# A retention and FP4 feed-forward kernel on one core: its opening, up to the third step, written out anew

## What is computed

```python
Q = _xpos(X @ W_Q);  K = _xpos(X @ W_K, downscale=True);  V = X @ W_V
scores = jnp.einsum('bqd,bkd->bqk', Q, K)
p_attn = jax.nn.softmax(scores, axis=-1) * 0.9 ** jnp.abs(n - m)
x = _layernorm(X + jnp.einsum('bqk,bkv->bqv', p_attn, V))

def fp4_quant_dequant(x):          # blocks of 16 along the last dim
    scale = jnp.maximum(jnp.max(jnp.abs(xb), axis=-1, keepdims=True) / 6.0, 1e-12)
    idx = jnp.searchsorted(_MID, jnp.abs(xb / scale))
    return _GRID[idx] * jnp.sign(xb / scale) * scale
# fp4_linear(x, w): einsum('bsk,nk->bsn', quantised x, quantised w)
h = jax.nn.silu(fp4_linear(x, w_gate)) * fp4_linear(x, w_up)
x = _layernorm(x + fp4_linear(h, w_down))
```

## Time and profile before

| | us |
|---|---|
| median of 3 runs (1080.03 to 1081.76) | 1081.22 |
| the profiled execution | 1081.23 |
| its span, from the first to the last instruction | 1079.4 |

### The profile page before, as it was taken

How to read it: one execution, slowest core, us unless ns; L and a number is a source line. 1 busy time by engine, 2 the same in 40 slices (tenths; PEclk the granted TensorE clock), 3 DMA queues, 4 the chain that set the end, 5 groups by cost and what they waited for, 6 DMA issues and landing times.

```text
span 1079.4 us, 20103 instructions
## 1 busy us (share of the span) xinstructions
PE 1017.5 (94%) x6756; PEld 950.8 (88%) x6756; DVE 888.1 (82%) x1762; ACT 577.0 (53%) x1395; POOL 753.6 (70%) x975
## 2 busy tenths in 40 slices
PE   5559999999999999999999999999999999999974
PEld 4448899999999999999999999999999999999964
DVE  6956888878888888888888888888888888888873
ACT  3233565556555565655555556645556565565543
POOL 3563786878777687868768687867767787666652
PEclk9769999999999999999999999999999999999987
DMA  5210010211012010211012010200111110000000
GB/s 189 81 63 26 11 59 21 69 40 60 16 36 79 20 55 16 80 40 51 19 41 78 12 59 21 78 31 20 60 40 54 35 60 20 16 20 21 21 11 20
DMA packets 28182, 47.24 MB, mean 44 GB/s; under 512 B 2864, under 2 KB 21552, under 8 KB 26032
## 3 DMA queue, kind: packets, MB, share of 16 engines
q1 hardware_dynamic: 27264, 45.17, 12.7%
q10 hardware_dynamic: 816, 0.79, 0.2%
HBM read 37.55 MB, written 8.39 MB: 43 GB/s over the span
## 4 chain that ended last, share of the span: by engine, by line
PE 86%; DVE 7%; issue 3%; POOL 1%; ACT 1%; DMA 1%; SPq 0%; POOLq 0%; DVEq 0%; ACTq 0%
PE ps_g L401 11%; PE ps_g L403 11%; PE ps_g L402 11%; PE ps_t L410 9%; PE ps_o L401 6%; PE ps_o L402 5%; PE ps_o L403 5%; PE ps_s L401 5%; PE ps_s L403 5%; PE ps_s L402 5%; PE ps_y L401 3%; PE ps_y L403 3%; PE ps_y L402 3%; PE ps_y L410 1%; DMA decay_t<-w_up 1%
## 5 line engine op out<-in xcount | busy, mean ns | idle before, releaser
L1291 POOL TENSOR_TENSOR h<-h,hsc 128x64 f32<-128x64 f32 (+3 forms) x257 | 204.0, 815 | 145.5 <-DVE h L1126 115.9
L401 PE MATMUL ps_g<-wgu_h,xqt_h 128*128 128x352 f32 x512 | 173.2, 338 | 2.7 <-DVE h L1097 1.7
L403 PE MATMUL ps_g<-wgu_h,xqt_l 128*128 128x352 f32 x512 | 165.6, 324 | 0.0
L402 PE MATMUL ps_g<-wgu_l,xqt_h 128*128 128x352 f32 x512 | 165.6, 323 | 0.0
L1455 POOL TENSOR_TENSOR prob<-prob,decay_t 128x512 f32<-128x512 f32 x128 | 162.8, 1292 | 3.1 <-ACT prob L782 3.1
L401 PE MATMUL ps_o<-v_h,pt_h 128*128 128x256 f32 x512 | 150.5, 294 | 5.8 <-DVE pt_l L962 5.8
L403 PE MATMUL ps_o<-v_h,pt_l 128*128 128x256 f32 x512 | 145.6, 284 | 0.0
L402 PE MATMUL ps_o<-v_l,pt_h 128*128 128x256 f32 x512 | 145.5, 284 | 0.0
L782 ACT ACTIVATE prob<-ps_s,nmax 128x1024 f32<-128x1024 f32 x64 | 71.3, 1114 | 87.0 <-DVE nmax L1158 87.0
L401 PE MATMUL ps_s<-k_h,q_h 128*128 128x512 f32 x256 | 107.6, 420 | 9.9 <-DVE k_l L1072 9.9
L1089 DVE SCALAR_TENSOR_TENSOR th<-th,ps_g 128x352 f32<-128x352 f32 x128 | 66.7, 521 | 57.4 <-ACT th L712 55.9
(11 more groups left out here) (195 smaller groups left out, 3072.7 us busy)
## 6 DMA issues: line engine op xcount, KB each, us to landing
rope_t<-rope SPq DMA_DIRECT2D x16, 1024.0 KB, 5.2
xin<-x_t SPq DMA_DIRECT2D x16, 512.0 KB, 4.0
xres<-x SPq DMA_DIRECT2D x64, 128.0 KB, 2.0
out<-yout SPq DMA_DIRECT2D x64, 128.0 KB, 1.7
decay_t<-decay SPq DMA_DIRECT2D x1, 960.0 KB, 4.8
h<-w_down SPq DMA_DIRECT2D x2, 352.0 KB, 4.5
prob<-w_k ACTq DMA_DIRECT2D x1, 256.0 KB, 3.3
prob<-w_q ACTq DMA_DIRECT2D x1, 256.0 KB, 4.9
```

Of the source, the lines that this page charges most:

```text
L401: pe.matmul(dst, a_h, b_h, start=(start and i == 0), stop=False)
L402: pe.matmul(dst, a_h, b_l, start=False, stop=False)
L403: mm = pe.matmul(dst, a_l, b_h, start=False, stop=(stop and i == n - 1))
L1291: return tt(blocks(dst), blocks(src), sc[:, which, at:at + n].unsqueeze(2).to_broadcast([P, n, QB]), ALU.mult)
```

## The change

The opening is written out anew up to the start of step 3. From there on each engine's instructions are the ones of before in the same order; the steps are now numbered straight through from 0 to 68 in place of a batch and a tile. What is new before step 3:

- Five homes in SBUF for the first loads, which share their bytes with halves of K and V that are written later (`sb_before` gives a tensor and frees its place at once): `w_first`, `w_last`, `w_down`, `rope_first`. The first sequence's K and V go into the other half (`half_of`). The first x chunk is split into `pt_h` and `pt_l`, the second is loaded into `x1`. SP issues all loads without a wait, gate and up rows of block 0 ahead of x.
- The weights are five blocks: 0, 1, 2 of 2 x 128 rows of gate and up (1024 columns, the last with 64 rows of padding), 3 and 4 of `w_down` (704 columns). POOL does all scalings of them.
- The magnitudes go to PSUM, into the two banks of `ps_o` and `ps_y`, now one tensor `ps_oy`. `wmag` is gone.
- The three first rotations have banks and buffers of their own (`ps_g`, `ps_s`, `ps_t`), the products with the sine stay in PSUM for two of them. DVE turns Q and the second K, POOL the first K; POOL makes all low parts of them.
- The weight transposes go to `ps_g`, in place of `ps_o` and `ps_y`, between the first scores, projections and value products.

```diff
-        w_buffers = [decay_t[:, 0:2 * D], decay_t[:, 2 * D:4 * D], x1_flat[:, 0:2 * D], x1_flat[:, 2 * D:4 * D],
-                     xin[:, 0], xin[:, 1], h[:, 0, 0:F], h[:, 1, 0:F]]
-        rot_borrowed = (prob[:].rearrange("p (a n) -> p a n", a=2), h[:, :, 0:CW])
-        w_magnitudes = [wmag[:], th_flat]
+        def sb_before(name, shape):
+            with nc.sbuf_tensor(name, shape, F32) as t:
+                return t
+        w_first = sb_before("first_gate_up", [P, 2, 2, 2 * D])
         k_h = sb("k_h", [P, 2 * DH * L], F32R)
+        w_last = sb_before("last_gate_up", [P, 2, 2 * D])
         k_l = sb("k_l", [P, 2 * DH * L], F32R)
+        w_down = sb_before("first_down", [P, 2, FP])
         v_h = sb("v_h", [P, 2 * NT * D], F32R)
+        rope_first = sb_before("first_rope", [P, 4, CW])
...
+        first_bank = (ps_g[:], ps_s[:], ps_t_pair)
+        first_cos = (rot_a[:], h[:, :, 0:CW], prob[:].rearrange("p (a n) -> p a n", a=2))
+        first_sin = (rot_b[:], ps_s[:], ps_t_pair)
+        def w_magnitude(m):
+            return ps_oy[:, :, 0:CW if m < 3 else FH]
+        def w_bank(g):
+            return ps_g[:, g % 2].rearrange("p (a n) -> p a n", a=4)
...
+            load_gate_up(0)
+            sp.dma_start(xin[:], x_chunks[0]).then_inc(first_x_arrived[0], 16)
+            load_gate_up(1)
+            sp.dma_start(first_table[0], rope[0][:, 2:4]).then_inc(first_rope_arrived[0], 16)
+            sp.dma_start(first_table[1], rope[0][:, 0:2]).then_inc(first_rope_arrived[1], 16)
+            load_last_gate_up()
+            sp.dma_start(rope_t[:], rope[1]).then_inc(rope_in, 16)
             sp.dma_start(ident[:], ident_in).then_inc(ident_arrived, 16)
-            load_chunk(Batch(0), 0)
-            sp.dma_start(rope_t[:], rope[0]).then_inc(rope_in, 16)
-            load_weights(0)
-            load_weights(1)
-            sp.wait_ge(xtl_done, 1)
-            load_chunk(Batch(0), 1)
...
+            sp.dma_start(w_down[:, :, 0:F], wd.rearrange("(u p) n -> p u n", p=P)).then_inc(w_arrived[3], 16)
             sp.dma_start(decay_t[:], decay).then_inc(decay_arrived, 16)
...
+            project(1, first_bank[0], first_xt[0], first_p_done[0])
+            pe.wait_ge(wqkvl_done, 2)
+            project(0, first_bank[1], first_xt[0], first_p_done[1])
+            pe.wait_ge(first_xl_done[1], 1)
+            project(1, first_bank[2], first_xt[1], first_p_done[2])
+            pe.wait_ge(wqkvl_done, 3)
+            pe.wait_ge(first_mul_done[0], 2)
+            values(first_v_bank[0], first_xt[0], first_p_done[3])
+            scores(0, 0)
+            pe.wait_ge(ident_arrived, 16)
+            weight_transposes(0)
+            weight_transposes(1)
+            scores(0, 1)
+            pe.wait_ge(first_rot_done[2], 2)
+            values(first_v_bank[1], first_xt[1], first_p_done[4])
+            pe.wait_ge(wtl_done, 2)
+            project_next(0, 1)
+            scores(1, 0)
+            scores(1, 1)
...
+            for s in range(OPEN, TILES + LAG):
+                step(s)
...
+            first_weight_high(0)
+            first_x_high(0)
+            weight_magnitude(0)
+            first_weight_high(1)
+            first_x_high(1)
+            first_weight_high(2)
...
+                wait(pe, xqtl_done, i + 1)
+                wait(pe, h_done, 2 * i + r)
```

More of the change, by code:

```diff
@@ L254, in build @@
         block = ctx.enter_context(nc.Block())
[L256 to L271, removed]
-                return 1, K_STEP[j], 1, 2 * K_STEP[j]
-            if j == 0:
-                return 0, 1, 0, 3
-            if j in Q_STEP and batch.has_next() and j > 0:
-                return 0, 0, 1, 1
-            return None
@@ L392, in _ @@
+            for s in range(TILES + LAG):
+                step(s)
             sp.wait_ge(out_stored, 16 * TILES)
@@ L514, in projection, with step @@
+            gate_up(0, 1)
+            def step(s):
+                now, prev, gu, dn, fin = (s - lag for lag in range(5))
+                rot, c_v = rotation(s), values_chunk(s)
+                def projection():
+                    wait(pe, h_done, 2 * dn + 2)
                     if rot is not None:
-                        which, c, on, _ = rot
-                        wait(pe, xtl_done, batch.lin(2, 2 * on + c + 1))
-                        project(which, k_done if which else q_done)
+                        project_next(*rot)
@@ L645, in weight_high, with weight_magnitude @@
+            def weight_magnitude(m):
+                act.wait_ge(wn_done, m + 1)
+                wait(act, wgrid_done, m)
+                nc.scalar.activation(w_magnitude(m), w_values(m), ACT.Abs, scale=MAGIC).then_inc(wabs_done, 1)
             def weight_high(g):
@@ L828, in step @@
+            rotated_high(0, 1)
+            probs_high(1, 0)
+            probs_high(1, 1)
+            x_magnitude(0)
+            exponential(2)
+            x1_high(0)
+            r1_mean(1)
+            r1_squares(1)
+            tanh(0, 0)
+            def step(s):
+                now, prev, gu, dn, fin, end = (s - lag for lag in range(6))
+                turned, c_v, c_x = rotation(s - 1), values_chunk(s), split_chunk(s)
+                urgent = rotation_is_urgent(s)
                 if c_v is not None and urgent:
@@ L1263, in _ @@
+                second_residual(fin)
+                x_max(prev)
+                h_low(dn)
+                x_scales(prev)
+            for s in range(OPEN, TILES + LAG):
+                step(s)
         @block.gpsimd
@@ new lines, in rotated_low @@
+            def rotated_low(which, c):
+                wait(pool, kqh_done, rotation_count(which, c) + 1)
+                if which:
+                    for a in range(DH):
+                        at = half_of(c // 2) * (DH * L) + a * L + (c % 2) * CW
+                        ins = tt(k_l[:, at:at + CW], rot_a[:, a, :], k_h[:, at:at + CW].bitcast(F32), ALU.subtract)
+                else:
+                    ins = tt(q_l[:, c % 2], rot_a[:], q_h[:, c % 2].bitcast(F32), ALU.subtract)
+                ins.then_inc(kql_done, 1)
```

1773 lines of the change are left out of this document (924 added, 849 removed).

## The result

| | before | after |
|---|---|---|
| median of 4 runs, us | 1081.49 (1080.03 to 1082.27) | 1055.59 (1054.66 to 1056.68) |
| profiled execution, us | 1081.23 | 1054.66 |
| its span, us | 1079.4 | 1052.8 |
| first score product of tile 3, us | 97.96 | 70.99 |
| from there to the end of the span, us | 981.4 | 981.8 |

The ratio is 0.9762, 95% interval 0.9745 to 0.9779: 25.9 us faster. Forecast were 1055.7 us and the range 1050 to 1065. The number is met; two of its terms, the start of step 3 and the stretch behind it, were off by some 2 us each, in opposite directions, as the experiments show. That it comes out within 0.1 us is in part luck.

What follows compares the result with a forecast made beforehand. The opening was taken as bound by the DVE and POOL chain quantising weights and rotating keys and queries, the body by PE. Step 3 moves from 97.96 to 72.5, so 1081.2 - 25.5 = 1055.7 us, range 1050 to 1065.

Steps and rivals of the forecast that it cites:

- the start of step 3: First score product of tile 3, ending the opening: 70.5 us by the sum, 72.5 with allowance, against 97.96 before.
- Loads: Start of the opening: x is split at 7.4 us instead of 5.73, a loss of 1.7; later loads cost nothing.
- The lock: Opening: POOL's operations hold DVE's with both inputs in SBUF; 4.4 us lost after 11.0, magnitudes in PSUM escape.
- Rival (a): Opening: POOL's locks catch DVE oftener, 8.3 us more, time 1064 us; chance 0.14.
- DVE's queue up to the row maximum: Opening from 11.0 us: 22.0 us of DVE work plus 4.4 lost behind POOL, ending at 37.4; scores whole by 36.3.
- Then POOL is last: Opening after DVE's last grid step at 49.6 us: POOL's 12.1 us of work sets the pace, to 61.8.
- The allowance of 2 us: Opening: waits without a visible cause, 3.5 us in the old chain, add 2 us, moving 70.5 to 72.5.
- The body: From tile 3's first score product to the end: same instruction orders, so the stretch stays at 981.4 us.
- rival (e): Body: an extra semaphore on each second gate and up product slows PE; 1086 us at 0.5 each; chance 0.02.
- Rival (c): Just after the opening: POOL and DVE arrive with work left, PE waits some 3 us, time 1059; chance 0.05.
- Rival (d): Opening: granted clock stays at 1.2 GHz, PE's 43.6 us become 87, time stays about 1081; chance 0.03.

Runs made afterwards that it cites:

- e5: The changed kernel with the first x chunk issued ahead of weight block 0 instead of behind it; 1060.42 us, median of three runs, ratio 0.9824.
- e1: The changed kernel with the magnitudes of the five weight blocks back in one SBUF buffer instead of PSUM; 1064.72 us, ratio 0.9853.
- e3: The changed kernel with the maxima of weight blocks 1 and 2 written to PSUM too; 1054.74 us, ratio 0.9762.
- e7: The changed kernel with POOL's second decay half of tile 1 cut to 16 of its 512 columns; 1056.76 us, ratio 0.9782.
- r0: The changed kernel measured once more, with no edit; 1056.05 us, ratio 0.9771.
- e4: The changed kernel with one wait fewer on the second gate and up product, tile 0 excepted; 1056.05 us, ratio 0.9769.
- e2: The changed kernel with its loads gated behind earlier work as before, and the second x chunk on SP's queue; 1066.39 us, ratio 0.9864.
- b1: The kernel before with only own homes and early loads for the eight weight blocks, order of work kept; 1080.52 us, ratio 1.0002.

## Why the prediction was right, and where it was not

- **Loads.** The direction was right and the size too small: x is split at 8.65 us, 2.9 later than before, not 1.7. The slices of the kernel after bring less at the start than those of the earlier trace rows (last columns: DMA share, GB/s):

```profile
1.75:3.50 1.75, 0.00 (x0) 0.00 (x0) 0.00 (x0) 0.69 (x1) 0.00 (x0) 1.00 0.71 158
3.50:5.25 1.75, 0.00 (x0) 0.00 (x0) 0.00 (x0) 0.98 (x2) 0.00 (x0) 1.00 1.07 378
```

  The prediction called the 16 DMA engines full there; its first row says 0.77, so the start is slower than the rate that it went on with. Block 0 is late as well (DVE begins at 5.92, 5.1 forecast), so POOL's scaling ends at 10.39 and not 9.8. The low part of x ends 1.1 us behind that, and PE starts 0.5 us late (11.61 against 11.1). An x that came earlier would meet the same scaling; e5 gained nothing by it, but delayed the weight block too, so it does not tell the two apart.
- **The lock.** That magnitudes in PSUM escape it and small scalings do not was right (e1, e3), and so was that it holds an operation until POOL is through rather than slowing both. Charged were 4.4 us behind 11.0; the kernel shows about 3.1 (1.0, 0.9 and 1.1 at the scales of blocks 1 and 2, the rest small). Rival (a), more hits, did not come.
- **DVE's queue up to the row maximum.** DVE is through by 36.6; the maximum waits 1.04 us more for the scores, which PE has at 37.6 and not by 36.3, since POOL's low part of Q lets PE go at 30.8 and not at 29.5. The two errors cancel: 37.67 against 37.4. This wait is all that DVE idles between the low part of x and the last grid step.
- **"Then POOL is last".** This is the step whose mechanism was wrong. The sum of POOL's work gave 61.8, and its low part of Q is done at 62.19, but e7 takes 1.1 us off POOL and nothing moves. Ahead of the reciprocal it is DVE that POOL waits for, and the sum itself held a wait of 0.4 us for DVE's scales; only the last two terms, units of x and low part of Q, are POOL's own. A sum of one engine's work that comes out right doesn't show that the engine is the bound; here the chains end together.
- **The allowance of 2 us** for waits without a cause was not needed. The bare sum, 70.5, was 0.5 short of 70.99 and within 0.3 of two later executions (70.51 in r0, 70.25 in e4). It was rounded up at each stage; its terms give 70.1 added without rounding.
- **The body.** "The orders of before and after agree ... apart from the semaphores that some of them wait for. So I leave the 981.4 us as they are" is the step that failed. One of these semaphores, on ACT, costs 7 x 0.41 us, and the stretch measured 983.5 us on average, not 981.4. I had weighed the semaphores on PE (rival (e)), not those of the engines that feed it. Rival (c), a gain given back, named the symptom but not the cause.
- **The clock.** Rival (d), a clock that stays at 1.2 GHz, did not come: 0.95 granted over the opening.

So the forecast of 1055.7 holds a surplus of 2 us in the opening and a missing 2 us in the body, and its closeness owes as much to this as to the sum. Of the 25.9 us gained, e1 and e2 say that magnitudes in PSUM carry 9 and early loads 11 in the new order, and b1 that the latter carry nothing in the old one. The two need not add up, and what the new order or the whole blocks would bring by themselves was not measured.

## What to carry to other kernels

- Where two programs agree in their order but not in their waits, compare the value of each changed wait on every engine, not only on the busiest: a stricter one on ACT, which is idle for half of the time, reached PE through DVE, once in 124 us.
- Where the profile names "issue" ahead of an operation, look up when its operands were written. It had started 0.11 us behind the last of them.
- To learn which engine bounds a stretch, take work away from it and see what waits instead. And a stretch that one profile shows unchanged is known only as well as it repeats, here 2 us.

## What the runs showed of the hardware

- A DVE operation with its inputs in SBUF stood for all that was left of POOL's two-input operation and then took 1.1 us more: 16.66 for POOL's end at 15.58, 38.08 for 36.99 (e1), 14.53 for 13.45 (e5). With one input in PSUM the grid steps took 0.88 (at 48.93) and 1.21 us (at 13.12) beside POOL in the kernel after. A scaling of 64 elements, with its one input in SBUF, was held as well, and took 0.21 for 1.23 us once that input lay in PSUM (e3).
- POOL was held in the same way by a DVE operation that had started first: 2.24 us for 1.39 (e1, at 38.50).
- Two transfers that swap their places in one queue do not swap their times: with x first, the split of x gained 2.3 us (8.65 to 6.39) and the first work on the weight block lost 3.1 (5.92 to 8.98), in one execution each.
- Two executions of the kernel after differ by 0.8 us in the last 30 us. From the transposes of the last x to those of h it is 6.71 us in the first (1022.14 to 1028.85) and 7.49 in r0 (1022.55 to 1030.04). The granted clock fell to 1.2 GHz behind the transposes of x in the first and ahead of them in r0, and was back at 2.4 GHz at 1026.3 and 1028.2 us.
